# Cross-attention and expert feed-forward on one core: the router's logits made from their PSUM bank, and new orders for all five engines in the attention

## What is computed

```python
def attend(ctx, latents, mask):              # latents = layernorm(x)
    xn, ln = layernorm(ctx), layernorm(latents)
    q = ln @ Wq.T
    k, v = split(concat([xn @ Wkv.T, ln @ Wlkv.T]))
    attn = softmax(mask(rmsnorm(q) * SCALE @ rmsnorm(k).T))
    return (attn @ v) @ Wo.T + bo
x = x + attend(ctx, layernorm(x), mask)

xf = layernorm(x).reshape(4096, 256)
logits = rmsnorm(xf) @ router_weight.T + router_bias      # 4096 x 16
probs = softmax(logits)
_, idx = top_k(logits.T, 256)                # per expert
y = gelu(xn[idx] @ fc1 + b1) @ fc2 + b2
x = x + scatter_add(y * probs[idx]) / sum_of_gates
```

## Time and profile before

| | us |
|---|---|
| median of 3 runs (lowest, highest) | 1110.83 (1109.19, 1113.75) |
| profiled execution, its own time | 1112.18 |
| its span in the trace | 1110.3 |
| PE busy in the span | 988.2 (89%), 6102 instructions |
| DVE busy | 807.4 (73%), 1925 |
| ACT busy | 677.2 (61%), 1352 |
| POOL busy | 769.0 (69%), 872 |
| mean granted clock of PE | 0.957 |

### The profile page before, as it was taken

One profiled execution on the slowest core, in us unless ns is written; L12 is line 12 of the kernel. 1 busy time (PEld: TensorE's weight loads), 2 busy tenths in 40 slices (PEclk: granted clock), 3 DMA queues, 4 the chain that ended last, 5 costly groups with the idle time before them and its releaser, 6 DMA issues.

```text
span 1110.3 us, 17756 instructions
## 1 busy us (share of the span) xinstructions
PE 988.2 (89%) x6102; PEld 653.9 (59%) x6102; DVE 807.4 (73%) x1925; ACT 677.2 (61%) x1352; POOL 769.0 (69%) x872
## 2 busy tenths in 40 slices
PE   3899999899999999999998999999821899999995
PEld 3655556455645645565565565444410789999995
DVE  7989858877777886787788678776678766666642
ACT  6855865667566766768666766544345346666662
POOL 4137986687887789588779958898503367777772
PEclk9899999999999999999999999999955799999998
DMA  6020020002002101110210010001055186666651
GB/s 184 1 62 1 2 62 20 1 1 65 1 1 80 41 1 43 45 41 2 63 41 1 1 47 1 2 1 52 2 162 171 24 180 201 201 201 201 200 161 22
DMA packets 73610, 71.82 MB, mean 65 GB/s; under 512 B 38928, under 2 KB 67568, under 8 KB 69424
## 3 DMA queue, kind: packets, MB, share of 16 engines
q1 hardware_dynamic: 66464, 61.92, 18.1%
q0 software_dynamic: 6272, 8.69, 4.5%
q10 hardware_dynamic: 784, 0.07, 0.1%
...
## 4 chain that ended last, share of the span: by engine, by line
PE 70%; DVE 10%; POOL 8%; ACT 4%; issue 3%; DMA 3%; SPq 0%; ACTq 0%; POOLq 0%; DVEq 0%
PE bank L913 39%; PE score_pair L913 16%; PE pair_bank L913 10%; POOL prob_sum L1500 8%; DVE c_in L1934 2%; ACT probs L1223 2%; PE bank L946 2%; PE bank L994 1%; DVE xe_lo L2103 1%; ACT xe_hi L1223 1%; DMA gathered<-rows_scratch,token_index 1%; DVE masked_scores L1813 1%; PE score_pair L1171 1%; DMA rows_scratch<-all_probs 1%; DMA v_nat<-in_w_lat 1%
## 5 line engine op out<-in xcount | busy, mean ns | idle before, releaser
L1500 POOL TENSOR_TENSOR prob_sum<-prob_sum,probs 128x256 f32<-128x256 f32 x628 | 467.0, 775 | 68.9 <-ACT probs L1223 62.0
L1223 ACT ACTIVATE probs<-score_pair,mask_col 128x512 f32<-128x512 f32 x256 | 162.1, 686 | 100.1 <-PE score_pair L913 91.0
L1813 DVE CUSTOM_DVE_ANT_0 masked_scores<-pair_bank,mask_bias 128x512 bf16<-128x512 f32 x248 | 160.5, 685 | 58.1 <-PE pair_bank L913 57.8
L913 PE MATMUL bank<-probs,v_nat 128*64 128x512 f32 x768 | 193.7, 611 | 0.0
L1223 ACT ACTIVATE probs<-score_pair 128x512 f32<-128x512 f32 x128 | 69.5, 595 | 76.0 <-PE score_pair L913 72.9
L1806 DVE TENSOR_REDUCE maxima<-pair_bank 128x2 f32<-128x1024 f32 x62 | 75.4, 1216 | 45.3 <-PE pair_bank L913 45.1
L913 PE MATMUL score_pair<-q_hi,k_hi 64*128 64x512 f32 x384 | 91.0, 466 | 10.2 <-ACT probs L1223 6.9
L913 PEld LDWEIGHTS bank<-probs,v_nat 128*64 128x64 f32 x768 | 45.4, 136 | 83.1 <-issue 80.1
L913 PE MATMUL pair_bank<-k_hi,q_hi 64*128 64x512 f32 x372 | 86.4, 457 | 4.3 <-DVE maxima L1806 2.3
L913 PEld LDWEIGHTS score_pair<-q_hi,k_hi 64*128 64x128 f32 x384 | 37.7, 184 | 80.1 <-ACT probs L1223 59.1
L1566 POOL DMA_INDIRECT out_x<-y_out,token_index x32 | 54.6, 1705 | 40.4 <-DVE y_out L2135 35.6
...
## 6 DMA issues: line engine op xcount, KB each, us to landing
...
```

The lines of the kernel that those rows point to most:

```text
L913: return pe.matmul(out, lhsT, rhs, start=start, stop=stop, skip_group_check=True)
L1223: return act.activation(out, a, f, bias=bias, scale=scale)
L1500: last = tt(total[:, half], first[:, half], p[:, half], ALU.add)
L1813: last = dve.tensor_tensor_reduce(masked[:, hh, :], place[:, hh, :], mask_bias[:, 512 * g:512 * (g + 1)], 1.0, MASKED, ALU.add, ALU.max, m ...
```

## The change

The multiplication of the logits now writes back into its PSUM bank, and the addition of the bias reads the bank and writes `logits_of(b)`. The bank is given free by the addition. `logits_scaled` is gone; its three readers wait for the bank's release. All other arithmetic, the instructions' number and their shapes stay, and so do the banks of the scores and maxima. All five tables have new times. 767 of PE's 896 attention pieces stand at another place in its order than before. What that does around one transition (batch 3, and with it 2, 4 and 5):

The diff, the tables cut to some of the entries named above:

```diff
--- before.py
+++ after.py
@@ -168,156 +168,156 @@
 TENSOR_TIMES = """
...
-v_lat.0:138865,75250,75031,75210,75167 qk.2:138669,67090,75065,53605,75069 qk.3:138679,67100,75072,75096,75086
...
-q.0:138914,75485,75273,75291,75477 k.0.0:138889,75450,75278,75280,75443 max.0.0.0:138942,75509,75329,75304,75484
...
-max.1.0.0:139091,119883,119799,119794,1063583 shift.0:139094,119881,119838,119819,1063587
...
-values.0.10:170633,170418,170421,170620,1063746 scores.1.0:170648,170451,170422,170629,1063740
-scores.1.1:170682,170551,170452,170691,1063752 den.0:170690,170511,170493,170702,1063753
-values.0.11:170690,170555,170495,170624,1063760 scores.1.2:170703,170570,170519,193414,1063761
...
-values.1.11:215058,215048,214983,1158748,1063885 den.1:215155,215094,215091,1158759,1063861
...
+qk.2:161896,88633,75242,75188,88917 v_lat.0:161924,88701,75252,75168,88948 qk.3:161907,88704,75255,75205,88924
...
+q.0:161976,98106,88699,75410,119738 k.0.0:161965,98148,88704,75419,89038 max.0.0.0:161978,98185,88722,88857,119802
...
+shift.0:162229,120063,119911,119961,1063573 max.1.0.1:162236,120124,119962,119982,1063615
...
+scores.1.0:193340,183870,183868,214905,1063776 scores.1.1:193353,184001,184010,214955,1063795
+values.0.11:193347,184129,184015,214947,1063806 den.0:193392,184057,184017,214958,1063797
...
+den.1:215286,215341,215334,1158775,1063936 out.2:215492,215512,215477,1158934,1063957
...
 VECTOR_TIMES = """
...
-stats_x:206949,111820,17208,16986,17010 kv.0:206981,112268,111971,82602,82576 kv.1:206994,112282,112043,112045,112258
...
-roots.0:206994,112400,155099,112476,112611 roots.1:207008,112411,155115,112485,177539
...
-row_max.0:207426,177729,177701,177686,207361 max.1.0.0:207445,207092,177730,177699,207379
...
-max.1.0.2:207467,207300,177760,207168,207404 first_roots.0:206940,,,, first_roots.1:206952,,,,
...
-max.1.3.2:272700,250242,250268,272707,207466 row_max.1:272707,250263,250278,272712,207470
-shift_rows.1:272719,250269,250300,272729,207481 recip.0.0:272761,250362,250357,272785,207484
...
-norm_o.1.1:302622,302411,302431,302584,1164937 out.2:302676,302647,302618,302630,1164942 end_roots.0:,,,302706,1164959
...
+stats_x:249644,154522,60100,60098,59878 kv.0:249695,154920,112304,112269,112248
...
+qk.3:249910,155273,155257,155264,155063 roots.0:249735,207201,155264,207052,207061
...
+max.0.3.2:250094,207424,207316,207319,207390 row_max.0:250096,207424,207391,207340,207395
...
+max.1.3.0:302384,250360,207679,250194,207521 first_roots.0:249622,,,, first_roots.1:249641,,,,
...
+row_max.1:302429,250444,250429,302272,207670 shift_rows.1:302430,302307,302302,302290,207760
...
+sum.1.11:,,,,1165032 end_roots.0:,,,1260122,1165100 end_roots.1:,,,1260141,1165101 end_roots.2:,,,1260173,1165126
...
 POOL_TIMES = """
...
-add_bias:396574,301580,378282,283169,782622 sum.0.6:396738,378292,378295,396689,782558
...
+sum.0.1:473410,378453,378455,378428,378429 add_bias:473406,378502,378465,283141,378324
...
 SYNC_TIMES = """
-w_ctx:-813770,,,, w_lat:-805640,,,, ctx.1:,191323,96188,96372,1314 ctx.0:,-10000095089,96203,1281,96388
-x:,-10000095091,96217,96386,1295 mask:-9999999920,191382,191341,191535,96488 x2:381862,476804,381845,286724,286754
-chunk:476818,477042,381899,381857, logits:476984,477040,477009,381881,286739 rows:571958,476999,477019,381895,286760
+w_ctx:-813770,,,, w_lat:-805640,,,, x:,191447,96307,1199,1250 ctx.1:,191458,96311,1241,1217
+ctx.0:,-10000095125,96312,96324,1190 mask:286578,191460,96336,96355,96360 x2:476892,381842,381787,286713,191650
+chunk:476952,476906,381826,286692, logits:476998,476912,381840,381808,191674 rows:476968,476917,381845,286797,286656
@@ -694,7 +694,7 @@
     last_added = signal("last_probs_added")
     o_copied, head_normed = signal("o_copied"), signal("head_normed")
     x_normed = signal("x_normed")
-    logits_scaled, centred_logits = signal("logits_scaled"), signal("logits_centred")
+    centred_logits = signal("logits_centred")
     soft_powers, gates_made = signal("soft_powers"), signal("gates_made")
     w_hi_made, w_lo_made = signal("expert_w_high"), signal("expert_w_low")
     rests_marked, ids_scaled = signal("list_rests_marked"), signal("list_ids_scaled")
@@ -744,8 +744,7 @@
 
     raised_by_vector = {"scale_qk": qk_scaled, "first_scale": qk_scaled, "scale_kc": kc_scaled, "max": max_emptied,
                         "row_max": row_max_made,
-                        "sum": last_added, "scale_logits": logits_scaled,
-                        "soft_max": centred_logits, "soft": gates_made}
+                        "sum": last_added, "soft_max": centred_logits, "soft": gates_made}
     for kind, *at in vector_plan:
         if kind in ("kv", "qk"):
             summed.will(kind, *at)
@@ -1090,7 +1089,7 @@
         def route_back(b):
             use = ("route_back", b)
             on.wait_ge(*misc.vacant(*use))
-            on.wait_ge(*logits_scaled.at(b))
+            on.wait_ge(*misc.emptied("route_logits", b))
             for j in range(MT):
                 if b < DIRECT:
                     last = pe.transpose(misc.bank(*use)[0:E, j * P:(j + 1) * P], batch_logits[:, j, :], ident[:])
@@ -1879,11 +1878,9 @@
                 on.wait_ge(*centred_logits.at(b - 1))
             elif b >= DIRECT:
                 on.wait_ge(*summed.at("qk", B - 1, MT - 1))
-            tt(logits_of(b), misc.bank(*use)[:, 0:MT * E].rearrange("p (j e) -> p j e", j=MT),
-               root_y[:, ROWS:N_ROOTS].unsqueeze(2).broadcast_to(shape), ALU.mult).then_inc(misc.empty(*use), 1)
-            on.wait_ge(*misc.emptied(*use))
-            tt(logits_of(b), logits_of(b), router_b[:].unsqueeze(1).broadcast_to(shape),
-               ALU.add).then_inc(logits_scaled.sem, 1)
+            made = misc.bank(*use)[:, 0:MT * E].rearrange("p (j e) -> p j e", j=MT)
+            settle(tt(made, made, root_y[:, ROWS:N_ROOTS].unsqueeze(2).broadcast_to(shape), ALU.mult))
+            tt(logits_of(b), made, router_b[:].unsqueeze(1).broadcast_to(shape), ALU.add).then_inc(misc.empty(*use), 1)
 
         def early_keys(b):
 
```

More of the change, by code:

```diff
@@ new lines @@
+max.1.3.2:193296,170452,170384,184144,1063746 scores.0.8:183927,170413,170429,184080,1063713
+values.0.5:183893,170383,170452,184113,1063696 values.0.6:183909,170436,170454,184116,1063718
+values.0.7:183909,170450,170454,184128,1063743 scores.0.9:193263,170457,170471,184149,1063723
+shift.1:193310,170489,170478,184180,1063759 scores.0.10:193295,170500,170479,184184,1063751
+values.0.8:193293,183814,170485,184185,1063756 values.0.9:193326,183815,170503,184186,1063764
+scores.0.11:193303,183832,170539,184187,1063762 values.0.10:193334,183830,183819,214927,1063773
@@ L297 @@
[L297 to L298 removed]
+stats_ctx.1:249634,154543,59844,59889,59853 stats_ctx.0:249617,154530,59873,60113,17024
+stats_x:249644,154522,60100,60098,59878 kv.0:249695,154920,112304,112269,112248
+kv.1:249705,154928,112305,112272,112357 kv.2:249737,154934,112353,112283,112423
+kv.3:249739,154945,112406,112308,112557 kv.4:249744,154947,112506,112459,112567
@@ new lines @@
+kv.5:249831,154955,112536,112510,112573 qk.0:249868,154966,155034,112485,112569
+qk.1:249894,155219,155197,112567,154991 kv.6:249839,155014,155221,112533,155052
+kv.7:249852,155246,155226,155258,155081 qk.2:249909,155225,155247,155013,155047
+qk.3:249910,155273,155257,155264,155063 roots.0:249735,207201,155264,207052,207061
+roots.1:249824,207206,207123,207074,207092 roots.2:249847,207218,207124,207075,207094
+scale_qk:,207232,207151,207146,207143 scale_kc.0:249745,207229,207153,207101,207124
+scale_kc.1:249900,207236,207161,207147,207117 prepare_q.0:249975,207258,207165,207162,207155
@@ new lines @@
+recip.1.2:302625,302678,302682,302633,1165048 recip.1.3:302732,302770,302732,302671,1165055
+norm_o.1.0:302730,302786,302755,302633,1165043 norm_o.1.1:302736,302796,302778,302891,1165071
+out.2:345306,345310,302825,1260110,1165091 out.0:302853,302821,302843,302683,1165080
+route_stats.0:345330,345549,302847,1260096,1165090 route_stats.2:345323,345512,345286,1260114,1165099
+scale_logits:397607,397614,397619,1260216,1165130 soft_max:397695,397696,397654,1260228,1165135
+soft:492634,492734,398019,1260232,1165136 early_keys:,,,,1164978 sum.1.9:,,,,1165024 sum.1.10:,,,,1165030
```

229 lines of the change are left out of this document (105 added, 124 removed).

## The result

Slower: 1115.35 us in the median (1112.53 to 1117.87), against 1110.83; ratio 1.0038, 95% interval 1.0026 to 1.0049. That is clear of the noise, outside the forecast range of 1096 to 1112, and inside what the prediction called "the same" (1105.3 to 1116.4). The profiled execution has a span of 1114.2 us, 3.9 more than before.

A forecast was written before the change was run, and what follows sets the result against it. PE bounds the middle (92.4 of 95.5 us a batch), DVE the start, POOL the end. Terms -1.5 +1.2 -1.0 +1.3 -2.0 -4.8 -1.3 = -8.1 gave 1104.1 from 1112.18, 1102.7 in the median's frame; forecast 1103.5, range 1096 to 1112.

The forecast's parts named there:

- part 2: Reordered attention from batch 2 on: -1.5 us for batches 2 to 5, then +1.2, -1.0 and +1.3 at other transitions.
- the new stall: PE at k.0.0, ahead of the second pair's first scores, waits 2.4 us for DVE's scales, 0.2 of it there before.
- one stall of 1.7, -1.0: At batch 6, den's wait of 2.0 and the shift's 0.6 make way for a single 1.7 us stall: -1.0 (-2 to +1).
- den's stall: PE's wait for POOL's sums before the denominators' matmul: 2.0 falls to 0.2 us in batches 2 to 5, -1.8 each.
- Rival (b): k.0.0's wait, with q and scores queued behind, becomes 5.4 us in each of five batches: 1119 us; chance 0.10.
- Start: More kv and qk tiles ahead of batch 0's first scores: -2 (-5 to +2); new column at 211 us: +1.2.
- Batch 7: PE's shift.6.1 moves earlier and row_max.6.1 later on DVE: a stall of 3.9 us, net +1.3 (-1 to +4).
- The end: POOL's and DVE's last sums of probabilities: shorter gaps and a faster first DVE sum, together -4.8 us (-5.5 to -2.2).
- The two gaps: POOL's waits of 2.03 and 2.40 us while den frees the sums' buffer would shrink: -1.45 and -1.2.
- POOL has 20 us to spare in that batch, so 0: add_bias.7, 2.38 us on POOL, moved into pair 6.0, would cost 0, at worst +1.3 us.
- The -2.15 on DVE: First of DVE's last three sums takes 1.29 instead of 3.44 us, as add_bias.7 no longer runs beside it.
- The gates: At the end, soft.7's 2.38 us wait for a DMA goes and DVE's own sequence remains: -1.3 us (-1.6 to 0).

The follow-up runs named there:

- squares_six: The changed kernel with the last squares moved earlier on PE, ACT and DVE in the transition from batch 5 to 6 alone; ratio to the kernel before 1.0039.
- fill: The changed kernel with 67 matmuls of 0.23 us added on PE ahead of its waits, nothing else; ratio to the kernel before 0.9985.
- bias_early: The kernel before with add_bias.7 moved ahead of sum.6.0.9 on POOL, nothing else; ratio to the kernel before 1.001.
- gates_early: The kernel before with the change's new order of the gates at the end, on DVE, PE, ACT and SP; ratio to the kernel before 0.998.
- bias_slack: The kernel before with add_bias.7 moved ahead of sum.6.0.5 on POOL, nothing else; ratio to the kernel before 0.998.

## Why the prediction was wrong

**The step that failed** is in part 2: a wait was priced by its length, and the clock behind it was put at nothing without a reason. The earlier trace rows has 1.00 for one batch, and I kept it there while I put stalls of 2.4 to 3.9 us into PE. The same table of before has another value two batches earlier, where the den stall of 2.3 us lies:

```profile
211.30:306.80 95.50, 92.64 (x523) 53.21 (x522) 70.18 (x172) 62.38 (x125) 73.91 (x96) 0.98 0.07 20
```

The runs show the changed kernel's holes of 1.6 to 4.9 us from 300 to 700 us followed by 3.4 to 6.8 us at 1.2 GHz in each transition (added up from the clocks of narrow windows); filled, 5.9 us come back. With 5.9 added, the forecast would have been 1109.4, "the same" by its own bounds. The other 6 us are in the sizes below.

**The sizes in part 2.** For batches 3 to 5 I put the new stall at 2.4; measured are 3.2, 1.6 and 4.1 (q and k together). DVE's chain, from qk.3's start on PE to scale_kc's first half, was 17.8, 16.1 and 18.6 us against a forecast of 17.3: right within 1.3. The transition to batch 6 was the worst: "one stall of 1.7, -1.0" became a stall of 4.9 and +6.5. With its hole filled it is +3.5, so 3.0 are the clock's and the rest is the chain's. I took batch 5's chain for it and looked neither at SP's order, where x.7's load stands 35 us later, nor at the maxima ahead of the roots, nor at ACT's exponential ahead of the last squares. den's stall went as forecast, in all batches.

The slowing beside POOL is real, as for the scales in the earlier trace rows. Roots of batch 6 on DVE, and POOL at that time, in after:

```profile
584.76 0.68 DVE L1589 TENSOR_SCALAR root_y<-root_w 128x80 int32<-128x80 int32 x1
586.91 0.78 DVE L1594 SCALAR_TENSOR_TENSOR root_t<-root_t,root_w 128x80 f32<-128x80 f32 x1
```

```profile
583.95 8.59 POOL L1499 TENSOR_TENSOR prob_sum<-prob_sum,probs 128x256 f32<-128x256 f32 x12 [1.46 <-ACT probs L1222]
```

The same in before, where POOL's sum begins in the middle of the roots:

```profile
578.68 0.20 DVE L1590 TENSOR_SCALAR root_y<-root_w 128x80 int32<-128x80 int32 x1
579.43 0.24 DVE L1595 SCALAR_TENSOR_TENSOR root_t<-root_t,root_w 128x80 f32<-128x80 f32 x1
579.71 0.81 DVE L1596 SCALAR_TENSOR_TENSOR root_y<-root_t,root_y 128x80 f32<-128x80 f32 x1
```

```profile
579.69 2.81 POOL L1500 TENSOR_TENSOR prob_sum<-prob_sum,probs 128x256 f32<-128x256 f32 x4 [3.18 <-ACT probs L1223]
```

0.20 to 0.24 us while POOL is idle and 0.68 to 0.81 beside its sums, for the same shape. Moving the chain trades one slow operation for another: the roots of batch 6 take 9.2 us in after and 8.1 in squares_six, where the scale of qk in turn took 3.4 instead of 2.4, and the chain ended at +20.3 and +20.6. The Trainium skill, "SBUF — State Buffer", section on SBUF's two separate sides, has it that the loser blocks for the whole instruction; the 0.2 that become 0.7, about one POOL instruction of 0.7, agree.

**Rival (b)** named the right mechanism, DVE's chain behind k.0.0, and the wrong price: it wanted a stall above 4.5 in five batches. It came above 4 in two; the clock added 7.2 us to all of them together, by fill's trace.

**Start**: -2 and +1.2 forecast, -2.7 and +1.3 measured. How much of the -2.7 is work moved into idle time is open, since up to scores.0.1.0 the granted clock is 0.94 in before and 0.97 in after. **Batch 7**: a stall of 3.9 forecast, 4.1 measured. That the net agrees (+1.3 and +1.4) is luck: with the hole filled the stretch is 1.8 us shorter, so the +1.4 contains a clock that the forecast had not.

**The end.** -4.8 forecast, -0.7 measured. Three terms fell. The two gaps (-1.45 and -1.2) did not shrink but grew by 0.65 and 0.1. den.6.1 in after shows why:

```profile
739.23 1.08 PE L912 MATMUL bank<-prob_sum,ones_col 128*64 128x512 f32 x4
```

It has no wait in brackets. POOL's last sum of pair 6.1 was done at 737.7 (740.40 less 2.68), but PE worked off a piece of maxima and scores.7.0.1 first, and den then took 1.08. The gap is PE's work in front of den, and taking values.6.1.11 from there left those two. And "POOL has 20 us to spare in that batch, so 0" for the bias addition was a mean over a batch put in place of the moment: bias_early lost some 2 us by it. The -2.15 on DVE came with 1.4 in bias_early, as the exponentials end just behind it.

**The gates**: -1.3 forecast, -3.3 in after's trace. gates_early's trace has -1.1 for that stretch, near the forecast. Much of the rest goes with the clock behind den.7.1, in before and in after:

```profile
796.00:800.00 4.00, 3.83 (x10) 1.44 (x12) 2.44 (x6) 0.00 (x0) 0.00 (x0) 0.57 0.08 8
```

```profile
803.50:807.50 4.00, 3.82 (x25) 2.52 (x26) 2.65 (x5) 2.16 (x5) 0.00 (x0) 1.00 0.00 0
```

In bias_slack, which has the old gates and 1.00 there, the stretch is 1.7 us shorter than before. So the forecast's term was about right, and the clock, at nothing here too, was missing in its favour.
